# A hybrid sequence model on one core: two sequences in each turn of the hardware loop

## The reference

```
x = x + attn_a(layernorm(x))   # conv(q,k,v) + silu, chunkwise delta rule, a short and a middle convolution of v, a router that mixes the four paths, Wo
x = x + ffn(layernorm(x))      # 64 slots: top-8 routing, gather, GRU update, scatter
x = x + attn_b(layernorm(x))   # causal softmax attention, 16 heads of 16
x = x + ffn(layernorm(x))      # the same ffn again
```

## Time and profile before

| | us |
|---|---|
| median of 3 runs | 8313.55 |
| lowest, highest run | 8311.75, 8318.34 |
| profiled execution: its own time | 8321.09 |
| profiled execution: span from first to last instruction | 8319.4 |
| PE busy | 7418.7 (89% of the span) |
| DVE busy | 4851.6 (58%) |
| ACT busy | 3369.7 (41%) |
| POOL busy | 1774.6 (21%) |
| mean granted TensorE clock | 0.942 |

### The profile page before, as it was taken

The page is one execution under the profiler, slowest core; times in us unless marked ns, Lnnn a source line. Parts: engine busy times, 40 slices in busy tenths (PEclk is TensorE's granted clock), DMA queues, the critical chain, the costliest instruction groups (busy, mean ns, idle before and its releaser), DMA issues. The chain is left out here.

```text
span 8319.4 us, 123018 instructions
## 1 busy us (share of the span) xinstructions
PE 7418.7 (89%) x48014; PEld 4312.9 (52%) x48014; DVE 4851.6 (58%) x9364; ACT 3369.7 (41%) x6883; POOL 1774.6 (21%) x2690
## 2 busy tenths in 40 slices
PE   6899988999889898899898998988999889998898
PEld 3546455464554645546455464554645546455464
DVE  5465654656646566565665646656466564666546
ACT  2252432525325253352533525335253442534425
POOL 2212221122211212112221122211222121221121
PEclk9999999999999999999999999999999999999999
DMA  3021210112112021120211202112021210212102
GB/s 73 18 34 28 37 41 21 33 25 37 41 23 43 13 37 41 28 40 15 32 41 29 39 15 32 41 34 44 6 32 41 37 41 6 32 41 37 41 10 33
DMA packets 337771, 268.59 MB, mean 32 GB/s; under 512 B 213521, under 2 KB 276369, under 8 KB 337097
## 3 DMA queue, kind: packets, MB, share of 16 engines
q1 hardware_dynamic: 337148, 260.09, 16.7%
HBM read 48.71 MB, written 42.02 MB: 11 GB/s over the span
## 5 line engine op out<-in xcount | busy, mean ns | idle before, releaser
L1814 DVE TENSOR_REDUCE sa_nm<-ps 128x2 f32<-128x1024 f32 (+4 forms) x1280 | 1393.5, 1115 | 388.9 <-PE ps L1799 198.5
L1889 ACT ACTIVATE pre<-ps 128x512 f32<-128x512 f32 (+3 forms) x3072 | 1272.3, 491 | 743.3 <-PE ps L1877 737.8
L1877 PE MATMUL ps<-sa_qs,sa_ks 99*128 99x512 bf16 (+3 forms) x3072 | 806.8, 337 | 136.6 <-DMA sa_qs<-sa_mrow 72.6
L1795 PE MATMUL ps<-sa_ks,sa_qs 96*128 96x512 bf16 (+3 forms) x2560 | 660.6, 332 | 82.8 <-DVE sa_nm L1814 68.9
L1896 POOL TENSOR_SCALAR_AFFINE_SELECT pre<-pre 128x512 f32<-128x512 f32 x512 | 325.0, 635 | 1766.6 <-ACT pre L1889 1764.2
L1909 PE MATMUL ps<-pre,sa_va 128*17 128x512 f32 (+3 forms) x6144 | 644.8, 491 | 8.2 <-POOL pre L1896 8.2
L1877 PEld LDWEIGHTS ps<-sa_qs,sa_ks 99*128 99x128 bf16 x3072 | 259.3, 98 | 715.8 <-ACT pre L1889 473.8
L318 PE MATMUL ps<-identb 128*128 128x512 bf16 x2320 | 583.2, 398 | 10.5 <-ACT dr_z L1153 10.5
L705 PE MATMUL ps<-rep,stack 128*32 128x512 f32 x4608 | 530.9, 613 | 33.7 <-DMA rep<-paths 33.7
L949 POOL TENSOR_TENSOR A<-paths 128x256 f32<-128x256 f32 x384 | 268.0, 726 | 792.3 <-DVE paths L1119 792.3
L1795 PEld LDWEIGHTS ps<-sa_ks,sa_qs 96*128 96x128 bf16 x2560 | 248.8, 101 | 269.0 <-DVE sa_nm L1814 98.5
(11 more groups left out here) (364 smaller groups left out, 14154.2 us busy)
## 6 DMA issues: line engine op xcount, KB each, us to landing
sa_qs<-sa_parts SPq DMA_DIRECT2D x288, 128.0 KB, 4.5
sa_ks<-sa_parts SPq DMA_DIRECT2D x288, 128.0 KB, 5.9
x<-in_x SPq DMA_DIRECT2D x17, 1024.0 KB, 5.6
rep<-paths SPq DMA_DIRECT2D x128, 128.0 KB, 2.7
bounce<-paths SPq DMA_DIRECT2D x32, 512.0 KB, 2.9
out_y<-x SPq DMA_DIRECT2D x32, 512.0 KB, 3.0
rep<-paths SPq DMA_DIRECT2D x128, 127.9 KB, 2.6
rep<-paths SPq DMA_DIRECT2D x128, 127.8 KB, 3.4
```

The lines of the kernel that those rows point to most:

```text
L1795: last = nc.tensor.matmul(cols[:, i, :], qs[0:NCOMB * AD, g % NBUF, op.j + i, op.t * P:(op.t + 1) * P], ks[0:NCOMB * AD, g % NBUF, op.j + ...
L1814: nc.vector.tensor_reduce(nm[:, g % 2, op.c, op.t, op.j:op.j + op.heads], cols, AX.X, ALU.max, negate=True).then_inc(s.slot_free, 1)
L1877: last = nc.tensor.matmul(bank[:, off:], ks[0:QROWS, g % NBUF, j, kt * P:(kt + 1) * P], qs[0:QROWS, g % NBUF, j, n * BANK + off:(n + 1) * ...
L1889: nc.scalar.activation(pt[:, gs % 2, j, off:BANK], ring_bank(ring_use(gs, j))[:, off:], ACT.Exp, scale=RATIO).then_inc(s.ring_out, 1)
```

## The change

The loop runs over 8 turns instead of 16, and its body holds the code of two sequences one behind the other. The input and the output are viewed as 8 groups of 2 sequences, and the two halves of the body take element `i` of the group `b`. Since the code of a stage is now emitted twice, each tensor gets a name of its own (`unused`); that is all the other edits do, in `setup`, `delta_rule`, `route`, `mix_and_project`, `slot_ffn`, `softmax_attention`, `sequence` and `build`.

```
+IN_TURN = 2
...
+USES = {}
+def unused(name):
+    USES[name] = USES.get(name, 0) + 1
+    return f"{name}_{USES[name]}"
...
-            return tmp.enter_context(nc.sbuf_tensor(name, shape, F32))
+            return tmp.enter_context(nc.sbuf_tensor(unused(name), shape, F32))
...
         next_x_view = w["x"].rearrange("b (t p) d -> b p t d", p=P)
-        y_view = y.rearrange("b (t p) d -> b p t d", p=P)
+        x_turns = w["x"].rearrange("(b i) (t p) d -> i b p t d", i=IN_TURN, p=P)
+        y_turns = y.rearrange("(b i) (t p) d -> i b p t d", i=IN_TURN, p=P)
...
-        with nc.Fori(0, SEQS) as b:
-            sequence(nc, k, ps, s, stacked, bounce, ones_rows, y_view[b], next_x_view[b])
+        with nc.Fori(0, SEQS // IN_TURN) as b:
+            for i in range(IN_TURN):
+                sequence(nc, k, ps, s, stacked, bounce, ones_rows, y_turns[i][b], x_turns[i][b])
```

More of the change, by code:

```diff
@@ L101, in sb @@
         def sb(name, shape, dt=F32):
-            return tmp.enter_context(nc.sbuf_tensor(name, shape, dt))
+            return tmp.enter_context(nc.sbuf_tensor(unused(name), shape, dt))
         taps = sb("su_taps", [P, (MID_STEPS + LOCAL_STEPS) * GROUPS])
@@ L2182, in sf @@
         def sf(name, shape):
-            return first.enter_context(nc.sbuf_tensor(name, shape, F32))
+            return first.enter_context(nc.sbuf_tensor(unused(name), shape, F32))
         paths = sf("paths", [P, PATHS, T, D])
@@ L2198, in sequence @@
             TT = pre[:].rearrange("p i a l -> p (i a l)")[:, 0:T * H * P].rearrange("p (t n) -> p t n", t=T)
-            A = inner.enter_context(nc.sbuf_tensor("A", [P, T, H * P], F32))
-            with nc.sbuf_tensor("rep", [P, GROUPS, PAD + L], F32) as rep:
+            A = inner.enter_context(nc.sbuf_tensor(unused("A"), [P, T, H * P], F32))
+            with nc.sbuf_tensor(unused("rep"), [P, GROUPS, PAD + L], F32) as rep:
                 project_and_convolve(nc, k, m, rep, pre, A, TT, bounce, ps, s["pc"], s["lc"], s["io"])
@@ L2212, in sb @@
         def sb(name, shape, dt=F32):
-            return ctx.enter_context(nc.sbuf_tensor(name, shape, dt))
+            return ctx.enter_context(nc.sbuf_tensor(unused(name), shape, dt))
         ps = ctx.enter_context(nc.psum_tensor("ps", [P, 8, BANK], F32))
```

## The result

| | us |
|---|---|
| before, median of 5 runs (8311.75 to 8330.64) | 8318.34 |
| changed, median of 5 runs (8273.23 to 8299.81) | 8282.81 |
| ratio changed to before, 95% interval | 0.9955 (0.9938 to 0.9973) |
| the unaltered changed kernel timed again beside before on another chip | 0.9950 (0.9937 to 0.9962) |

The change makes the kernel 0.45% faster, that is 0.0045 x 8318 = 37 us, with an interval from 22 to 52. "First sequences" are those that begin at a back edge, "second sequences" those that begin at a seam inside the body.

The account below looks back on a forecast made before the run. PE's stream with its waits was taken to set the pace, PE and DVE pausing for instructions at each back edge. Eight seams at 6.0 us gave 48, from the runs' median of 8313.55 to 8265 us, range 8243 to 8292.

Parts of the forecast that it names:

- The pauses: At 8 of 15 back edges the instruction fetch goes; the value projection begins about 0.2 us behind the barrier, not 4.3.
- The clock behind the pause: Behind the seam PE keeps full clock, so the value projection takes 7.1 us instead of 9.56, 2.4 us gained.
- DVE sets the last piece: At ACT's L752, DVE's convolutions set the start: 17.0 us behind the seam instead of 23.0, so 6.0 a seam, not 6.5.
- 4.9 in, 5.0 out: The first turn, 4.9 us ahead at L752, ended 5.0 shorter, so the seam's gain was taken to reach the turn's end.
- The costs taken at nothing: Longer body: POOL or SP may fetch code at the 7 remaining back edges, at most 4.2 us each; taken as nothing.
- The sum against the profiled execution: Whole kernel: 8 seams x 6.0 = 48 us off the profiled execution's 8321.1, giving 8273.
- Rival 3: Seam code is fetched as slowly without a branch, so no change: 8313 to 8315 us; chance 0.08.
- rival 4: SP must fetch its code mid-sequence, ahead of its copies into `rep`: 18 us slower, 8331 us; chance 0.06.
- Rival 2: Wait at L705 moves to where the clock is not lowered; second sequences 505.3, gain 75 us, 8238; chance 0.09.
- Rival 1: Fetch goes but the clock gives back less, or second sequences fall on 512.1: gain 21 to 34, 8279 to 8293; chance 0.19.

Follow-up runs that it names:

- the announced back edge: Kernel before, loop of 16 one-sequence turns, with the loop option telling all engines of the back edge ahead of it: ratio 0.9948 to before.
- the held seam: Changed kernel with PE alone made to wait about 4.2 us at the inner seams for four GpSimd memsets: ratio 1.0001 to before.
- PE alone freed: Kernel before with the back edge announced on PE only, by a loop written out by hand: ratio 0.9988 to before.
- DVE alone: Kernel before with the back edge announced on DVE only, by a loop written out by hand: ratio 1.0003 to before.
- four in a turn: Four sequences in each of four turns instead of the changed kernel's two in each of eight: ratio 0.9920 to before.
- the second profile: Profile of the changed kernel run once more, unaltered, beside before on another chip: ratio 0.9950 to before.
- the cold kernel: Changed kernel without the eight warm products that end each sequence's last stage: ratio 0.9928 to before.

## Why the prediction was right, and what of its size was off

The sign was right and the time within the range: 8282.8 us in 8243 to 8292, against 8265 forecast. The gain was 37 us (22 to 52) and not 48. Part of the 17.8 us between 8265 and 8282.8 is that before itself was at 8318.3 in this comparison and not at the 8313.6 that I started from.

- **The pauses.** Eight of fifteen are gone, 0.3 us stands on PE there, and the compare-and-branch shows 8 times, once at 79 ns. Right. That the fetch behind the branch makes the pause is shown by the announced back edge, which removes it without touching the body.
- **The clock behind the pause.** 2.4 us were forecast; the projection went from 9.56 to 7.10 us at 1.00. Right, and the held seam shows that the pause does it, whatever causes it.
- **DVE sets the last piece.** L752 was to begin 17.0 us behind the seam and began at 16.5, right behind the SiLU that waits for DVE. With PE alone freed it is 20.2, with DVE alone 23. Right; the seam is worth 6.5 at this place, not 6.0.
- **"4.9 in, 5.0 out".** I passed the gain at L752 through to the turn's end one to one, on the evidence of one turn, and took 508.7 for a second sequence. Where no activation is late that held: four in a turn has 508.6 on average for its third and fourth sequences. In the changed kernel the first stage kept the gain (6.7 us), but the attention and the last stage gave back 2.3, so that 515.4 became 511.0.
- **The costs taken at nothing.** This is the term that was mis-sized. I asked what longer code would cost and looked at POOL and SP at the back edges; they were not late, and that part was right. What the second copy of the code cost was on ACT, in the middle of the attention: two activations 0.28 us late each, 0.6 us at the stage's end and 1.7 more by the clock's second fall, 2.3 us in each of eight sequences, 18 us. The first turn of before could not show it, as its copy of the code has no late activation. The seven back edges left cost 0.3 us more each on PE (32.7 / 7 against 65.7 / 15) and 0.8 on DVE.
- **The sum against the profiled execution.** Second sequences took 8 x (511.45 - 508.7) = 22 us more than forecast, of which the 18 above; the rest is scatter from sequence to sequence. The very first sequence took 3.5 more (513.9 against 510.4 before), the seven other first ones 7 x (514.93 - 514.7) = 1.6. That makes 27, against the 26.5 us by which the profiled span misses the 8319.4 - 48 = 8271.4 that the forecast gives. By the ratio the gain misses the forecast by less, 48 - 37 = 11 us, since this execution was a slow one of its kind.
- **The rivals.** Rival 3 (no change) and rival 4 (slower) are out. Rival 2 (505.3) was not seen in the changed kernel: its shortest second sequence is 508.5 (507.7 in the second profile). Rival 1 has the measured number in its span, but not by its mechanism: at the seam the clock stood at 1.00, and the sequence ended 1.1 us below the step of 512.1, since with two in a turn the steps are those of the whole turn. What I had not on my list was that a copy of the same code can be slower than its neighbour.

What stays open: whether the border between two packets of instructions is what makes the activations late (a run that only moves ACT's code by some instructions would tell), what makes the clock fall a second time in the three sequences without them, and why the turns come in steps of 3.4 us.

## What to carry to other kernels

A pause of PE can cost more than its length, by what the clock takes behind it, whichever of a fetch or a wait makes it. Look for "issue" rows at a loop's head before looking at the body, and announce the back edge on every engine that meets there, since freeing one only moved the wait here. When a body is doubled, compare the two copies stage by stage: the same code was 2.3 us slower in one copy, from two instructions late by 0.28 us each. Before blaming such a loss on the earlier start, look for a copy that starts as early without the loss (four in a turn), and for one that starts late and has it (the held seam).

## What the runs showed of the hardware

- A taken back edge of this loop showed 3.7 to 4.7 us on PE's branch, and DVE stood 5 to 6 us before its next instruction; announced ahead, 0.94 us on PE. The Trainium skill, page "Runtime: NRT & Kernel Launch", section on instruction fetch mechanics, says that the branch out of the pages at hand forces a fetch; the trace agrees, and the packets of instructions are not saved by the announcement (399 against 414 on q8, 177 against 209 on q14), only the time.
- Pauses of 1.41 and 1.03 us, 1.09 us of work between them, were followed by a clock of 0.50, and pauses of 1.10 and 1.03 at the same place were not. One of 1.72 us at the seam was followed by a fall too, one of 0.3 never. The length of the pause alone does not decide: behind 2.04 us at L715 the clock fell, and behind 2.21 at the same place in the cold kernel it did not; with PE alone hinted, three of fifteen pauses of 2.1 to 2.7 us passed without a fall.
- An activation came 0.28 us late at two places, 128 of ACT's recorded instructions apart, in every pass of one copy of the code and in no pass of its neighbour.
- The same code at the same kind of seam takes 508.5 to 514.3 us from sequence to sequence, with equal instruction counts: a difference of a few microseconds in one sequence of one profile says nothing here, and stages have to be compared over all sixteen.
